# Cross-attention value product in 64x32 tiles over two PSUM banks, with new positions for feature-table, load and cross/FFN units

## The chip, the cores and the metric

One core of a Trainium2 chip runs the kernel; the other cores are idle. The metric is device microseconds (us) of one execution, and the time given for a kernel is the median of its executions. Engines: TensorE (PE; PEld is its weight load), VectorE (DVE), ScalarE (ACT), GpSimd (POOL) and SyncE (SP), which here only starts DMAs.

## The reference

One decoder layer on x of shape (4, 512, 256) in float32, with a context of 64 rows per batch part. Cut to what matters:

```python
def feature_map(x, fm_w, fm_b):                       # cross attention only
    z = einsum('nshd,ed->nshe', x, fm_w) + fm_b
    return concatenate([exp(z), exp(-z)], axis=-1)    # 16 -> 32 per head
def self_attention(x):                                # H=16 heads, key 16, value 64
    q = einsum('bnd,hkd->bnhk', x, query_proj); k = ...; v = ...
    attn = softmax(einsum('bnkh,bmhk->bnhm', q, k) / 4, axis=1)
    return einsum('bnhv,dhv->bnd', einsum('bnhm,bmhv->bnhv', attn, v), output_proj)
def cross_attention(ctx, query):                      # 16 heads of 16, 64 context rows
    v, k, q = (feature_map(t, fm_w, fm_b) for t in (ctx, ctx, query))
    attn = softmax(einsum('nqhd,nkhd->nhqk', q, k) / 16, axis=-1)
    out = einsum('nhql,nlhd->nqhd', attn, v)          # the product that is changed
    return out.reshape(N, S, 512) @ fc_w.T + fc_b
def ffn(x):                                           # x_prev is x shifted by one row
    xr = mu_r * x + (1 - mu_r) * x_prev; xk = mu_k * x + (1 - mu_k) * x_prev
    return sigmoid(xr @ W_r) * (relu(xk @ W_k) ** 2 @ W_v)
x = x + self_attention(layernorm(x))
x = x + cross_attention(ctx_1024, layernorm(x))
x = x + ffn(layernorm(x))
```

## The kernel before

**Units and orders.** The work is cut into units with a name, a batch part b (0 to 3) and arguments. Each engine runs its own list of units strictly in order, and the engines meet through semaphores. A list comes from hand-kept tables of slots: `orders()` gives each unit one slot per engine that has a share in it and sorts by slot. Self attention is 64 quads, q = 0 to 63, sixteen per batch part; a quad is two heads against half of the keys, its units have the slots 16q plus the numbers of `ATTENTION`: `scores` (PE), `max` (DVE), `exp` (four on ACT), `rsum` (DVE), `scale` (POOL, scales V by the row sums), `weigh` (PE, product with V), and for each second quad `ot_hi` (ACT) and `ot_lo` (DVE). Between them stand the other units. `PLAN` says where for every batch part (256 slots each; the offset -1 puts a unit of part b among the quads of part b+1), `FIRST` and `ONCE` for part 0's start, `LAST` for part 3's cross attention and FFN, which have no quads beside them, and `DEFER` for those units of part 2 that don't follow `PLAN`.

**Loads of the stacks.** q and k of a batch part are made in four `qk` units: (c, o) with c the half of the heads and o = 0 for q, 1 for k. PE makes one, ACT and DVE split it into a high and a low part in `qkt_hi`, `qkt_lo`, and SP writes both to DRAM (`q_parts`, `k_parts`; L547). From there `ld` (b, p) reads a stack of one pair of heads into `q_st` (L559) and `k_st` (two DMAs, L563). `scores` of an even quad waits for the stack n = q/2, so quads 14, 30, 46 and 62 wait for `ld` (b, 7). ACT's share of a `qk` unit waits until the q or k before it has been written out, as `qkt_hi` is one buffer. SP is in order too: if its next unit waits, all later DMAs wait behind it.

**Cross attention.** `t2` transposes the normalized rows, `z` and `xs` make features and scores with 64-row tiles of the array, two at a time into two PSUM banks; DVE takes maxima, ACT exp, DVE sums (`xn`), POOL scales, `pt` transposes (PE, then ACT copies to `pt_sb`). `pv` is the value product: `vblk` holds for a pair of heads a block-diagonal 128x64 matrix, so that one matmul serves two heads with 128 rows by 64 columns of the array, and two matmuls lie side by side in the columns. It is done per half of the rows and per group gg of heads. ACT (`oxt_hi`) and DVE (`oxt_lo`) split its result and `fc` multiplies it with the output weights.

**PSUM.** `scores` has four banks, `weigh` one (which has the same 128x64 tile form as `pv`), all other PE units go round the three left (seven when no scores are due); `bank_uses` deals them in PE's order.

**Feature tables.** `load("feat")` brings the small matrix and bias in ten DMAs; `feat` on DVE and ACT makes the signed table and its high and low parts. `cut` splits weights into high and low parts; the low part of the output weights, `cut("o")`, is made on POOL (L1319), and V of the second half of the heads may not be copied to `v_sb` before it, since the raw weights lie there.

## Time and profile before

| | |
|---|---|
| median of 3 executions | 479.99 us (479.38 to 481.4) |
| profiled execution, its own time | 479.61 us |
| span in the trace | 477.8 us |
| busy share of PE, DVE, ACT, POOL | 93%, 79%, 63%, 28% |
| scores of quads 0, 9, 28 and 63 start | 26.7, 67.5, 183.2 and 404.9 us |
| POOL first adds the `fc` bias | 122.3 us |

The span is the time from the first to the last instruction in the trace; 1.8 us of the execution's time lie around it. Times of rows are counted from the span's start. PE overlaps its matmuls, so a record's duration has some 0.17 us of latency that the next one doesn't add.

### The profile page before, as it was taken

What the parts mean: (1) busy time and instruction counts of PE and PEld (TensorE: products, weight loads), DVE (VectorE), ACT (ScalarE), POOL (GpSimd) and SP (SyncE); (2) the same over time, 40 slices, a digit from 0 to 9 for tenths busy, and PEclk for the clock granted to TensorE, in tenths of its full rate; (3) what the DMA queues carried; (4) which work ended last, traced back from release to release, by engine and by line L of the source; (5) the groups of instructions that cost most, each with busy time, mean ns of one, the idle gap of its engine ahead of it and who ended that gap; (6) DMA issues with size and microseconds to landing.
All of it is one profiled execution on the core that took longest, in us unless ns stands there. A gap on an engine that the chain in (4) does not pass through costs nothing.

```text
span 477.8 us, 7930 instructions
## 1 busy us (share of the span) xinstructions
PE 445.1 (93%) x2588; PEld 276.3 (58%) x2588; DVE 379.9 (79%) x689; ACT 299.0 (63%) x732; POOL 134.5 (28%) x181
## 2 busy tenths in 40 slices
PE   7779979999999999999999999999999999896985
PEld 3553426535655676557565675566556664485774
DVE  6567676786999988886999989777999787669664
ACT  4348866577688756565796856655796668323431
POOL 2511113113623351214431442114332413142410
PEclk9979999999999999999999999999999999897999
DMA  7852210133221001323301301333102000000001
GB/s 257 309 173 108 78 68 18 45 110 123 101 86 59 12 1 34 114 68 119 105 26 47 105 6 45 113 116 118 59 16 77 36 2 0 23 0 23 2 1 44
DMA packets 20013, 34.02 MB, mean 71 GB/s; under 512 B 2308, under 2 KB 6660, under 8 KB 19844
## 3 DMA queue, kind: packets, MB, share of 16 engines
q1 hardware_dynamic: 19972, 33.52, 21.5%
q8 instruction: 21, 0.34, 0.3%
q14 instruction: 20, 0.16, 0.1%
...
## 4 chain that ended last, share of the span: by engine, by line
PE 75%; DVE 9%; issue 5%; ACT 5%; DMA 3%; POOL 1%; SPq 0%; ACTq 0%; DVEq 0%; POOLq 0%
PE av_bank L653 18%; PE m_bank L591 9%; PE m_bank L593 7%; PE m_bank L592 7%; PE s_pair L639 7%; ACT e_sb L862 4%; DVE nmax L1060 3%; PE m_bank L782 3%; PE m_bank L831 3%; DMA q_parts<-qkt_lo 3%; PE m_bank L795 3%; PE m_bank L770 2%; PE m_bank L820 2%; PE av_bank L603 2%; PE m_bank L670 2%
## 5 line engine op out<-in xcount | busy, mean ns | idle before, releaser
L862 ACT ACTIVATE e_sb<-s_pair,nmax 128x512 f32<-128x512 f32 x256 | 172.8, 690 | 55.9 <-DVE nmax L1060 55.9
L1060 DVE TENSOR_REDUCE nmax<-s_pair 128x2 f32<-128x1024 f32 x128 | 152.9, 1214 | 20.2 <-PE s_pair L639 19.3
L653 PE MATMUL av_bank<-e_sb,v_sb 128*64 128x512 f32 x512 | 124.5, 607 | 4.5 <-POOL v_sb L1330 2.4
L1330 POOL TENSOR_TENSOR v_sb<-v_sb,rsum 128x256 f32<-128x256 f32 x64 | 39.6, 619 | 179.3 <-DVE rsum L1068 169.5
L653 PEld LDWEIGHTS av_bank<-e_sb,v_sb 128*64 128x64 f32 x512 | 31.6, 136 | 57.8 <-issue 46.6
L639 PE MATMUL s_pair<-q_st,k_st 64*128 64x512 f32 x256 | 50.6, 457 | 9.5 <-issue 6.8
L862 ACT ACTIVATION_READ_ACCUMULATOR e_sb<-s_pair,nmax 128x1 f32 x256 | 53.4, 208 | 0.0
L639 PEld LDWEIGHTS s_pair<-q_st,k_st 64*128 64x128 f32 x256 | 21.2, 186 | 55.3 <-issue 35.0
L1357 POOL TENSOR_TENSOR sx<-sx,xrec 128x512 f32<-128x512 f32 x24 | 24.8, 1043 | 46.4 <-DVE xrec L1240 46.4
L591 PE MATMUL m_bank<-wo_hi,ot_hi 128*128 128x256 f32 x120 | 34.9, 291 | 0.0
L593 PE MATMUL m_bank<-wo_lo,ot_hi 128*128 128x256 f32 x120 | 33.5, 279 | 0.0
L592 PE MATMUL m_bank<-wo_hi,ot_lo 128*128 128x256 f32 x120 | 33.5, 279 | 0.0
L875 ACT ACTIVATE ot_hi<-av_bank 128x512 fp32r<-128x512 f32 x32 | 19.3, 603 | 16.9 <-PE av_bank L653 16.8
L1068 DVE RECIPROCAL rsum<-esum 128x4 f32<-128x4 f32 x64 | 10.9, 170 | 22.1 <-ACT e_sb L862 21.4
L591 PE MATMUL m_bank<-wv_hi,xt_hi 128*128 128x512 f32 x62 | 27.9, 451 | 0.0
L591 PEld LDWEIGHTS m_bank<-wo_hi,ot_hi 128*128 128x128 f32 x120 | 22.5, 187 | 6.2 <-issue 6.1
L1339 POOL TENSOR_TENSOR rstd<-veps,power 128x2 f32<-128x2 f32 x24 | 16.7, 697 | 30.2 <-DVE veps L1124 30.2
L593 PE MATMUL m_bank<-wv_lo,xt_hi 128*128 128x512 f32 x62 | 25.0, 404 | 0.0
L592 PE MATMUL m_bank<-wv_hi,xt_lo 128*128 128x512 f32 x62 | 24.9, 402 | 0.0
L995 ACT ACTIVATE pt_sb<-m_bank 128x512 f32<-128x512 f32 x30 | 17.7, 598 | 10.3 <-PE m_bank L782 9.9
L1072 DVE TENSOR_TENSOR ot_lo<-av_bank,ot_hi 128x512 fp32r<-128x512 f32 x32 | 21.8, 681 | 1.7 <-ACT ot_hi L875 1.7
L592 PEld LDWEIGHTS m_bank<-wo_hi,ot_lo 128*128 128x128 f32 x120 | 22.5, 188 | 0.1
...
## 6 DMA issues: line engine op xcount, KB each, us to landing
...
```

The lines of the kernel that those rows point to most:

```text
L591: pe.matmul(dst, a_hi, b_hi, start=first, stop=False)
L592: pe.matmul(dst, a_lo, b_hi, start=False, stop=False)
L593: return pe.matmul(dst, a_hi, b_lo, start=False, stop=last)
L639: mm = pe.matmul(s_pair[i][:, par, :], k_st[at, n % STACK, m * P:(m + 1) * P], q_st[at, n % STACK, :], start=True, stop=True)
L653: mm = pe.matmul(av_bank[n % AV_BANKS][64 * par:64 * par + 64, :], v_sb[:, m, 2 * p + par, :], e_sb[:, (4 * q + 2 * i + par) % E_RING, :], ...
L862: act.activation(e_sb[:, g % E_RING, :], s_pair[k // 2][:, k % 2, :], ACT.Exp, bias=nmax[:, g % 8:g % 8 + 1], accum_out=esum[:, q % 4, k:k ...
L875: act.activation(ot_hi[:, n % 4, :], av_bank[n % AV_BANKS][:, :], ACT.Copy).then_inc(ot_hi_ready, 1)
L995: act.activation(pt_sb[:, 4 * gg:4 * gg + 4, (t % 2) * P:(t % 2 + 1) * P], bank(unit)[:, :].rearrange("p (i n) -> p i n", i=4), ACT.Copy)\
L1060: dve.tensor_reduce(nmax[:, at:at + 2], s_pair[i][:, :, :], AX_X, ALU.max, negate=True)\
L1072: dve.tensor_tensor(ot_lo[:, n % 4, :], av_bank[n % AV_BANKS][:, :], ot_hi[:, n % 4, :].bitcast(F32), ALU.subtract)\
L1330: pool.tensor_tensor(v_sb[:, m:m + 2, 2 * p:2 * p + 2, :], v_sb[:, m:m + 2, 2 * p:2 * p + 2, :], rsum[:, q % 4, :].rearrange("p (m h) -> p ...
L1357: pool.tensor_tensor(sx3, sx3, xrec[:, n % 4, :].unsqueeze(2).broadcast_to([P, 8, L]), ALU.mult)\
```

## The change

`pv` is done per half alone, in tiles of 64 rows by 32 columns: a head has its own 64x32 block of `vblk`, which no longer holds zeros, the heads of the upper 64 rows go to one bank and those of the lower 64 rows to another, and four column tiles lie side by side in each. So a half takes 16 matmuls of 64x32 in place of 8 of 128x64, and the unit waits for both banks and for all four `pt` copies of its half. The `fc` weights are permuted on the host to match. The filler matmuls (`warm`) at the start have 256 columns in place of 512. All tables have new slots. In the order of the units this does, beside many small swaps: `feat` goes from ahead of quad 0 to behind `max` of quad 4 on DVE; `load("rest")` (a batch part of x, biases, FFN weights, 1.4 MB) and `load("x1")` go from the start of SP's list to later places; `ld` (0, 2) comes before the DMAs of `qk` (0; 1, 0) and no longer after; `ld` (b, 7) comes behind the DMAs of `qk` (b+1; 0, 0) and no longer before; `cut("o")` goes behind `scale` of quad 2 on POOL; `ot_lo` goes ahead of both `max` units of its quad; `fv` (2, 0) goes behind `weigh` of quad 62 on PE; the fillers at the end are placed ahead of the last `xs` units. `DEFER` now lists all cross and FFN units of part 2.

```diff
...
 PLAN = [
-    ("qk", 0, (1, 0), dict(pe=5, act=1, dve=4, sp=14)),
...
-    ("kv", -1, (), dict(pe=-25, dve=-27)),
+    ("qk", 0, (1, 0), dict(pe=3, act=-3, dve=-3, sp=-7)),
...
+    ("kv", -1, (), dict(pe=-57, dve=-55)),
...
-    ("pv", -1, (0, 0), dict(pe=134, act=128, dve=125)),
...
-    ("pv", -1, (0, 1), dict(pe=136, act=129, dve=134)),
...
-    ("ld", 0, (7,), dict(sp=178)),
...
-    ("fk", -1, (0,), dict(pe=236, act=247, pool=239)),
-    ("qk", 1, (0, 0), dict(pe=206, act=207, dve=206, sp=230)),
...
-    ("qk", 1, (0, 1), dict(pe=223, act=221, dve=220, sp=235)),
...
+    ("pv", -1, (0, 0), dict(act=126, dve=123)),
...
+    ("pv", -1, (0,), dict(pe=134)),
+    ("pv", -1, (0, 1), dict(act=126, dve=129)),
...
+    ("ld", 0, (7,), dict(sp=219)),
...
+    ("fk", -1, (0,), dict(pe=227, act=234, pool=230)),
+    ("qk", 1, (0, 0), dict(pe=214, act=195, dve=211, sp=201)),
...
+    ("qk", 1, (0, 1), dict(pe=221, act=224, dve=223, sp=222)),
...
 LAST = [
...
-    ("pv", (0, 0), dict(pe=1081, act=1049, dve=1184)),
...
-    ("pv", (0, 1), dict(pe=1196, act=1152, dve=1231)),
...
+    ("pv", (0, 0), dict(act=1446, dve=1422)),
...
+    ("pv", (0,), dict(pe=2087)),
+    ("pv", (0, 1), dict(act=1452, dve=1437)),
...
 DEFER = [
...
-    ("fv", (0,), dict(pe=7, dve=-2, sp=5)),
...
+    ("op", (1, 0), dict(pe=-221, dve=-220)),
...
+    ("pv", (0, 0), dict(act=-122, dve=-116)),
...
+    ("pv", (0,), dict(pe=-117)),
+    ("pv", (0, 1), dict(act=-113, dve=-113)),
...
+    ("fv", (0,), dict(pe=15, dve=38, sp=15)),
...
 FIRST = [
-    ("warm", (0, 2), dict(pe=-1187)),
...
-    ("first", (0,), dict(pe=-282, act=-235, dve=-282)),
-    ("first", (1,), dict(pe=-126, act=-128, dve=-77)),
-    ("qk", (0, 0), dict(dve=-620, sp=-615, pe=-617, act=-561)),
-    ("qk", (0, 1), dict(pe=-376, act=-368, dve=-413, sp=-375)),
...
-    ("ld", (1,), dict(sp=-111)),
-    ("load", ("o",), dict(sp=-1334)),
-    ("ld", (2,), dict(sp=17)),
-    ("load", ("x1",), dict(sp=-1)),
-    ("load", ("fc",), dict(sp=-355)),
-    ("load", ("rest",), dict(sp=-2172)),
-    ("load", ("feat",), dict(sp=-822)),
...
+    ("warm", (0, 2), dict(pe=-210)),
...
+    ("first", (0,), dict(pe=-191, act=-194, dve=-181)),
+    ("first", (1,), dict(pe=-105, act=-103, dve=-116)),
+    ("qk", (0, 0), dict(dve=-842, sp=-229, pe=-155, act=-864)),
+    ("qk", (0, 1), dict(pe=-146, act=-151, dve=-149, sp=-140)),
...
+    ("ld", (1,), dict(sp=-130)),
+    ("load", ("o",), dict(sp=-1880)),
+    ("ld", (2,), dict(sp=-12)),
+    ("load", ("x1",), dict(sp=174)),
+    ("load", ("fc",), dict(sp=-773)),
+    ("load", ("rest",), dict(sp=259)),
+    ("load", ("feat",), dict(sp=-1357)),
...
 ONCE = [
-    ("cut", ("o",), dict(act=-195, pool=-202)),
...
-    ("feat", (), dict(dve=-190, act=-192)),
-    ("kf", (0,), dict(pe=57, act=73)),
...
-    ("warm", (3, 1), dict(pe=1751)),
-    ("warm", (4, 1), dict(pe=2626)),
...
+    ("cut", ("o",), dict(act=14, pool=52)),
...
+    ("feat", (), dict(sp=87, dve=84, act=83)),
+    ("kf", (0,), dict(pe=156, act=149)),
...
+    ("warm", (3, 1), dict(pe=1903)),
+    ("warm", (4, 1), dict(pe=3038)),
...
-ATTENTION = dict(scores=12, weigh=42, max=(11, 12), exp=(17, 17, 18, 18), rsum=27, scale=22, ot_hi=39, ot_lo=44)
+ATTENTION = dict(scores=13, weigh=42, max=(11, 11), exp=(16, 16, 17, 17), rsum=26, scale=15, ot_hi=36, ot_lo=43)
...
 def bank_units(name, b, args):
-    if name in ("xs", "z"):
+    if name in ("xs", "z", "pv"):
...
-        vblk = sb("vblk", [P, NP, 2 * FE])
+        vblk = sb("vblk", [P, NP, FE])
...
-                cols = 512 if at < 3 else 256
+                cols = 256
...
-                    pe.matmul(av_bank[0][:, 0:cols], id_sb[:, :] if at >= 3 else vblk[:, 0:2, :].rearrange("p a b -> p (a b)"),
+                    pe.matmul(av_bank[0][:, 0:cols], id_sb[:, :] if at >= 3 else vblk[:, 0:4, :].rearrange("p a b -> p (a b)"),
...
-            def pv(b, half, gg):
-
-                unit = ("pv", b, (half, gg))
-                wait_bank(pe, unit)
+            def pv(b, half):
+
+                units = bank_units("pv", b, (half,))
+                for unit in units:
+                    wait_bank(pe, unit)
...
-                    wait_emptied(pe, ("pt", b, (t, gg)))
+                    for gg in range(2):
+                        wait_emptied(pe, ("pt", b, (t, gg)))
...
-                    for q in range(2):
-                        pair = 4 * gg + 2 * i + q
-                        mm = pe.matmul(bank(unit)[64 * q:64 * q + 64, i * HALF:(i + 1) * HALF], vblk[:, pair, :],
-                                       pt_sb[:, pair, :], start=True, stop=True)
-                mm.then_inc(filled[uses[unit][0]], 1)
+                    for c in range(4):
+                        for r, unit in enumerate(units):
+                            rows = slice(64 * r, 64 * r + 64)
+                            mm = pe.matmul(bank(unit)[32 * c:32 * c + 32, i * HALF:(i + 1) * HALF],
+                                           vblk[rows, 4 * i + c, :], pt_sb[rows, 4 * i + c, :], start=True, stop=True)
+                            if (i, c) == (1, 3):
+                                mm.then_inc(filled[uses[unit][0]], 1)
...
-                    wait_filled(act, ("pv", pb, (ph, gg)))
+                    for r in range(2):
+                        wait_filled(act, ("pv", pb, (ph, r)))
...
-                    wait_filled(dve, ("pv", b - 1, (1, 1)))
+                    for r in range(2):
+                        wait_filled(dve, ("pv", b - 1, (1, r)))
...
-                    ins = dve.tensor_copy(to[64 * q:64 * q + 64, :, :, q * FE:(q + 1) * FE],
+                    ins = dve.tensor_copy(to[64 * q:64 * q + 64, :, :, :],
...
-    wfc = np.asarray(L0_xattn_fc_w).T.reshape(2, 2, 2, 2, FE, D).transpose(2, 0, 1, 3, 4, 5).reshape(H * FE, D)
+    wfc = np.asarray(L0_xattn_fc_w).T.reshape(4, 2, 2, FE, D).transpose(2, 1, 0, 3, 4).reshape(H * FE, D)
...
```

## Rows read from the trace of the kernel before

**Rows 1.** The page: busy time of the engines (share of the span) and records.

```profile
PE 445.1 (93%) x2588; PEld 276.3 (58%) x2588; DVE 379.9 (79%) x689; ACT 299.0 (63%) x732; POOL 134.5 (28%) x181
```

**Rows 2.** Busy time by stretch: stretch, length, engines, PE clock, DMA share, GB/s.

```profile
5.00:10.00 5.00, 5.00 (x15) 2.41 (x14) 3.71 (x14) 2.36 (x5) 1.43 (x2) 1.00 0.95 350
...
45.00:90.00 45.00, 39.60 (x198) 19.84 (x192) 31.50 (x51) 32.37 (x90) 8.99 (x15) 1.00 0.14 47
...
180.00:285.00 105.00, 104.89 (x642) 66.09 (x641) 91.03 (x168) 71.27 (x180) 32.99 (x46) 1.00 0.22 71
```

**Rows 3.** Waits of PE from 90 to 390 us: total, times, longest; the longest line.

```profile
PE m_bank L770 <- issue: 0.6, 1, 0.6
```

**Rows 4.** Timeline of PE: a 64-row unit, the V product, scores.

```profile
128.48 1.16 PE L770 MATMUL m_bank<-kblk,qf 64*128 64x128 f32 x16
129.57 1.94 PE L653 MATMUL av_bank<-e_sb,v_sb 128*64 128x512 f32 x8
131.44 0.73 PE L639 MATMUL s_pair<-q_st,k_st 64*128 64x512 f32 x4
```

**Rows 5.** Timeline: a value product (one half) and the V product behind it.

```profile
164.66 2.04 PE L795 MATMUL m_bank<-pt_sb,vblk 128*64 128x256 f32 x16
...
166.50 1.92 PE L653 MATMUL av_bank<-e_sb,v_sb 128*64 128x512 f32 x8
```

**Rows 6.** Timeline of SP in part 1: the second q write.

```profile
187.59 0.61 SPq L547 DMA_DIRECT2D q_parts<-qkt_lo  x1
```

**Rows 7.** Busy time by stretch, chosen for DMA traffic (share and GB/s at the end).

```profile
150.10:151.30 1.20, 1.20 (x12) 0.75 (x11) 1.20 (x2) 1.20 (x3) 0.35 (x1) 1.00 0.00 0
151.30:158.50 7.20, 6.42 (x52) 3.75 (x49) 6.66 (x11) 5.31 (x14) 1.04 (x1) 1.00 0.23 75
...
188.10:192.00 3.90, 3.90 (x22) 2.33 (x19) 3.79 (x12) 2.22 (x6) 1.26 (x2) 1.00 0.46 134
...
197.00:211.00 14.00, 14.00 (x66) 8.69 (x65) 10.06 (x14) 8.30 (x22) 2.22 (x3) 1.00 0.22 72
```

**Rows 8.** Timeline of PE: scores of quad 30, and of quad 14.

```profile
195.12 1.11 PE L639 MATMUL s_pair<-q_st,k_st 64*128 64x512 f32 x4
...
97.90 0.51 PE L639 MATMUL s_pair<-q_st,k_st 64*128 64x512 f32 x2
```

**Rows 9.** Timeline of SP from 86 to 108 us: the first q write of part 1.

```profile
90.11 0.63 SPq L547 DMA_DIRECT2D q_parts<-qkt_hi  x1
```

**Rows 10.** Timeline of the start, all engines.

```profile
20.17 4.50 POOL L1319 TENSOR_TENSOR wo_lo<-v_sb,wo_hi 128x2048 fp32r<-128x2048 f32 x1 [1.11 <-ACT wo_hi L905]
...
20.82 3.94 DVE L1173 TENSOR_SCALAR fm_sb<-fm_sb 128x128 f32<-128x128 f32 x1 [2.89 <-DMA fm_sb<-in_fm_t]
...
26.74 1.22 PE L639 MATMUL s_pair<-q_st,k_st 64*128 64x512 f32 x4 [6.17 <-issue]
...
28.25 0.60 SPq L547 DMA_DIRECT2D q_parts<-qkt_lo  x1
...
38.03 0.61 ACT L930 ACTIVATE qkt_hi<-m_bank 128x512 fp32r<-128x512 f32 x1
...
39.51 0.69 ACT L862 ACTIVATE e_sb<-s_pair,nmax 128x512 f32<-128x512 f32 x1 [0.87 <-DVE nmax L1060]
```

**Rows 11.** Timeline of PE at the end of the quads.

```profile
406.04 1.99 PE L842 MATMUL m_bank<-wffn_sb,kact 128*128 128x256 f32 x8
...
411.87 2.58 PE L653 MATMUL av_bank<-e_sb,v_sb 128*64 128x512 f32 x8 [1.98 <-POOL v_sb L1330]
414.38 3.00 PE L831 MATMUL m_bank<-mix_k,wffn_sb 128*128 128x256 f32 x8
```

**Rows 12.** Busy time by stretch: the clock there.

```profile
412.90:416.40 3.50, 3.50 (x11) 1.70 (x8) 1.20 (x3) 0.60 (x1) 0.00 (x0) 0.52 0.00 0
```

**Rows 13.** Timeline of ACT: the two halves of the first value product of part 3.

```profile
446.94 0.60 ACT L1006 ACTIVATE oxt_hi<-s_pair 128x512 fp32r<-128x512 f32 x1 [0.89 <-PE s_pair L795]
447.81 0.60 ACT L1006 ACTIVATE oxt_hi<-s_pair 128x512 fp32r<-128x512 f32 x1 [0.27 <-PE s_pair L795]
```

More of the change, by code:

```diff
@@ new lines @@
+    ("pt", -1, (3, 1), dict(pe=183, act=171)),
+    ("ln1", 1, (0,), dict(dve=178, pool=160)),
+    ("pv", -1, (1, 0), dict(act=178, dve=184)),
+    ("ln3", -1, (0,), dict(dve=171, pool=180)),
+    ("ld", 0, (6,), dict(sp=175)),
+    ("pv", -1, (1,), dict(pe=186)),
+    ("pv", -1, (1, 1), dict(act=178, dve=184)),
+    ("t1", 1, (0,), dict(pe=190, act=188, dve=193)),
+    ("mix", -1, (0,), dict(dve=206)),
+    ("t3", -1, (0,), dict(pe=205, act=194)),
+    ("ln1", 1, (1,), dict(dve=182, pool=161)),
@@ new lines @@
+    ("xs", (0, 0), dict(dve=516, act=445)),
+    ("z", (1, 0), dict(act=366)),
+    ("xs", (0,), dict(pe=971)),
+    ("xs", (0, 1), dict(dve=523, act=539)),
+    ("xn", (0, 0), dict(dve=1307, pool=34)),
+    ("xs", (1,), dict(pe=1084)),
+    ("xs", (1, 1), dict(dve=1051, act=1040)),
+    ("xn", (1, 0), dict(dve=1321, pool=1301)),
+    ("xn", (0, 1), dict(dve=1309, pool=34)),
+    ("z", (1,), dict(pe=1380)),
+    ("z", (1, 1), dict(act=444)),
+    ("xs", (1, 0), dict(dve=554, act=570)),
+    ("xn", (1, 1), dict(dve=1352, pool=1301)),
@@ new lines @@
+    ("xs", (2, 0), dict(dve=1308, act=1312)),
+    ("pt", (0, 0), dict(pe=2052, act=606)),
+    ("pt", (0, 1), dict(pe=2056, act=1364)),
+    ("xs", (2,), dict(pe=2005)),
+    ("xs", (2, 1), dict(dve=1308, act=1444)),
+    ("xn", (2, 0), dict(dve=1354, pool=1345)),
+    ("xs", (3,), dict(pe=2032)),
+    ("xs", (3, 1), dict(dve=1389, act=1510)),
+    ("pt", (1, 1), dict(pe=2087, act=1430)),
+    ("xn", (2, 1), dict(dve=1389, pool=1392)),
+    ("xs", (3, 0), dict(dve=1372, act=1491)),
+    ("pt", (1, 0), dict(pe=2064, act=1395)),
@@ new lines @@
+    ("z", (0,), dict(pe=-196)),
+    ("z", (0, 1), dict(act=-195)),
+    ("z", (0, 0), dict(act=-197)),
+    ("xs", (0, 0), dict(dve=-186, act=-187)),
+    ("z", (1, 0), dict(act=-158)),
+    ("t2", (1,), dict(pe=-162, act=-163, dve=-162)),
+    ("xn", (0, 0), dict(dve=-181, pool=-168)),
+    ("xs", (1, 0), dict(dve=-177, act=-173)),
+    ("xs", (0,), dict(pe=-188)),
+    ("xs", (0, 1), dict(dve=-185, act=-181)),
+    ("xn", (1, 0), dict(dve=-154, pool=-163)),
+    ("pt", (1, 0), dict(pe=-133, act=-132)),
@@ new lines @@
+    ("xn", (0, 1), dict(dve=-160, pool=-166)),
+    ("z", (1,), dict(pe=-149)),
+    ("z", (1, 1), dict(act=-155)),
+    ("pt", (0, 0), dict(pe=-142, act=-155)),
+    ("xs", (1,), dict(pe=-175)),
+    ("xs", (1, 1), dict(dve=-170, act=-167)),
+    ("pt", (1, 1), dict(pe=-126, act=-132)),
+    ("xn", (1, 1), dict(dve=-153, pool=-153)),
+    ("xn", (2, 0), dict(dve=-135, pool=-138)),
+    ("xs", (2,), dict(pe=-140)),
+    ("xs", (2, 1), dict(dve=-146, act=-129)),
+    ("pt", (0, 1), dict(pe=-141, act=-150)),
@@ new lines @@
+    ("pt", (3, 0), dict(pe=-88, act=-94)),
+    ("pt", (3, 1), dict(pe=-88, act=-94)),
+    ("pv", (1, 0), dict(act=-94, dve=-79)),
+    ("pv", (1,), dict(pe=-75)),
+    ("pv", (1, 1), dict(act=-81, dve=-79)),
+    ("fc", (0,), dict(pe=-94, dve=-95)),
+    ("ln3", (0,), dict(dve=-91, pool=-92)),
+    ("mix", (0,), dict(dve=-61)),
+    ("t3", (0,), dict(pe=-70, act=-72)),
+    ("ln3", (1,), dict(dve=-27, pool=-28)),
+    ("fc", (1,), dict(pe=-66, dve=-39)),
+    ("t3", (1,), dict(pe=-6, act=-6)),
@@ new lines @@
+    ("warm", (1, 2), dict(pe=-2414)),
+    ("warm", (2, 2), dict(pe=-2370)),
+    ("ln1", (0,), dict(dve=-2197, pool=-2055, do=-2061)),
+    ("ln1", (1,), dict(dve=-2108, pool=-2000, do=-2059)),
+    ("cut", ("first",), dict(act=-2072, dve=-2059)),
+    ("cut", ("qk",), dict(act=-2049, dve=-2000)),
+    ("t1", (0,), dict(dve=-2058, pe=-2091, act=-2057)),
+    ("t1", (1,), dict(pe=-2035, act=-2041, dve=-2054)),
+    ("first", (0,), dict(pe=-191, act=-194, dve=-181)),
+    ("first", (1,), dict(pe=-105, act=-103, dve=-116)),
@@ L230 @@
+    ("v", (0, 1), dict(pe=19, dve=21)),
+    ("v", (0, 2), dict(pe=-108, act=-126)),
+    ("v", (0, 3), dict(pe=32, dve=34)),
 ]
 ONCE = [
[L233 to L241 removed]
```

292 lines of the change are left out of this document (127 added, 165 removed).

## The prediction, made before the change was run

> **What bounds the kernel now.** The page first: PE is busy for 93% of the span, DVE for 79%, ACT for 63% [rows 1]. The average hides stages, so the second view is busy time by stretch: from 180 to 285 us, a whole part of the batch, PE is busy for 104.9 of 105 us, DVE for 91.0; in part 0 (45 to 90 us) PE has 39.6 of 45 [rows 2]. The view of waits says the same: from 90 to 390 us the longest entry of PE is 0.6 us [rows 3]. So in parts 1 to 3 whatever PE saves comes off the end, whatever PE is made to wait goes onto it, and no other engine matters until it makes PE wait. The start and the end of the span are chains of waits and are read from timelines.
>
> **1. The value product.** One half has 16 matmul records in a group of 2.04 us, and the V product behind it ends at 168.42, 1.72 us after the end of the value product [rows 5]; it has four rounds of two records side by side with 512 columns, so a round of 512 columns takes 0.43 and one of 256 takes 0.215. The value product has eight rounds now: 1.72 us. If eight 64x32 tiles run side by side, its 32 records are four rounds: 0.86. That saves 0.86 us per half, and the six halves of parts 0, 1 and 2 lie beside quads, in the PE-bound stretch: -5.2. The two of part 3 lie in the end, where the next step is ACT's copy. Now the first group is copied at 446.94 while PE makes the second, copied at 447.81 [rows 13]; afterwards both banks are full only at the end of the unit and the copies follow one another, so fewer rounds are paid back by less overlap: 0, between -0.5 and +0.9 a half. Bounds of the whole term: -5.2 if eight run together, 0 if four do. Two side by side in the columns are seen for the value product, two in the rows for `xs` [rows 4, 5]; eight are seen nowhere. I take eight, since both directions work one by one and nothing in the rows shows them competing.
>
> **2. Changes of tile form.** A group with 64-row tiles ends at 129.64 and the V product after it at 131.51, 1.87 us later [rows 4], against 1.72 where the value product with the same form stood ahead [rows 5]: 0.15 us for the change. Scores after it end at 132.17, 0.66 later, of which 0.43 are their two rounds: 0.23. The value product has a form of its own now, so it can't share one with `weigh`. Putting both orders side by side from the tables, PE changes form 213 times from quad 0 to quad 62 before and 207 times after, because more units of one form stand together: six fewer at 0.18 is -1.1. Bounds -1.4 and 0. The Trainium skill (TensorEngine Tiling (Array Packing), section Tiling Modes) says that a change of mode drains the engine; by that rule a form used by one unit alone is a cost, and the 0.15 to 0.23 us here agree with it.
>
> **3. The last stack of each part.** `ld` (b, 7) goes behind the two q writes of the next part. What it then costs is seen from three things. First, when SP can issue: it is in order, and the second q write of part 2 goes out at 187.59 [rows 6]; its two writes move from 188.1 to 192.0. Second, how long a stack takes: alone, from issue at 150.1, nothing moves for 1.2 us and then data moves for 7.2 us; two stacks close behind each other take 14.0 [rows 7]. So 7.0 each, and it follows at 192.0: it lands at 199.0, and at about 199.5 because `t3` now stands ahead of that `qk` unit on PE. Third, when it is needed: quad 30's scores start at 195.12 [rows 8]; with `fk` moved in ahead (a group of eight such records is about 1.9 us, as in [rows 11]) and the short `kv` moved out (about 0.5) at 196.4. PE waits 3.1 us, and everything behind it on PE too: it is in order, and this stretch has no idle time to give. The same for quad 46: 6.2 together. For quad 14 the first q write goes out at 90.11 [rows 9]: traffic from 91.3, 3.9 for the writes and 7.0 for the stack, 102.2 against 97.90 [rows 8]; 4.3, of which I take 4.0, as part 0 has idle time of its own. Sum +10.2. Before, this load was issued long ahead (at 150.1 for a need at 195.1), so it is covered fully now. Bounds: 0, if the stack needn't wait behind the writes, and +15, if each wait also lets PE's clock fall: a wait of 1.98 us at 409.9 was followed by 3.4 us at half clock [rows 11, 12], worth up to 1.7 us each.
>
> **4. The start.** Now DVE's step of `feat` takes 3.94 us beside POOL's 4.50 us step of `cut("o")`, the unit `first` (0, 1) waits behind it, and PE idles 6.17 us, to 26.74 [rows 10]. With `feat` gone that idle time goes too, and quad 0 starts some 6 us sooner. I don't expect it to last. ACT's share of `qk` (0; 1, 1) stands between the exps of quads 1 and 2 and can't start until the q write of `qk` (0; 1, 0) has landed. Now that write is issued at 28.25 and ACT gets to the unit at 38.03 without waiting [rows 10], so it landed between about 33 (4.7 us after its issue, as in [rows 6, 7]) and 38. Afterwards the stack `ld` (0, 2) is ahead of it: +7.0 [rows 7]. What is taken out ahead of it is 1.4 + 0.5 MB, at 350 GB/s [rows 2] 5.5 us. So it lands between 34.5 and 39.5, and the exps of quad 2 start at 35 to 40 where they started at 39.51: about -1.5 from there. Against it stand two things. The low part of the output weights (4.50 us on POOL) comes behind quad 2's `scale`, and DVE's copy of `v` (0; 1, 1), with the maxima of quad 4 behind it, waits for it: about +1.3. And `feat` on DVE and ACT, which wait for each other there, stands in the loop of quad 4: about +1.2. Together +1.0; bounds -6.2 (the idle time is gained for good) and +3.
>
> **5. The end of the quads.** `weigh` of quad 63 waits 1.98 us for POOL, the clock falls, and `fk` takes 3.00 us where a like group takes 1.99 [rows 11, 12]. With `fv` (2, 0) in that gap PE idles less; the chain to `weigh` itself is unchanged. If the clock stays up: 1.0 for `fk` and 0.6 for `weigh` (2.58 against 1.94, [rows 4]); I take -1.5, bounds -1.6 and 0. In part 3's cross attention the fillers no longer stand between the `pt` units but ahead of them, which frees the path but may leave the clock low: -0.5, bounds -2 and +2.
>
> Edits with no cost of their own: `load("rest")` is needed by POOL at 122.3 us and would be issued at about 110, behind the writes of `qk` (1; 1, 0); it has slack as long as it moves at the 350 GB/s of [rows 2] (4 us). The narrower fillers and `ot_lo` ahead of `max` move work by tenths.
>
> **Sum.** -5.2 - 1.1 + 10.2 + 1.0 - 1.5 - 0.5 = +2.9, against the profiled execution's 479.6 (477.8 in the span and 1.8 around it; the median of the runs is 0.4 higher): **482.5 us**.
>
> **Rivals.** *B, the stacks come in time.* It decides at the 3.1 us of quad 30: if a stack behind a q write lands within 8 us of the second write's issue and not 11.9, term 3 is zero and the time 482.5 - 10.2 = 472.3. For it: 16 DMA engines are only 22% busy while a stack moves [rows 7], so a second transfer could run beside it. Against it: two stacks took 14.0, exactly twice one. *C, the tiles don't pack.* If records of the value product follow one another as those of `xs` do, 16 in the 1.09 us from 128.48 to 129.57 [rows 4], 32 take 2.2 us, no less than now: term 1 becomes about +0.5, the time 488.2. For it: no row shows more than two at once. Against it: both pairings that the rows show, two in the columns and two in the rows, run at the full rate of a round. The Trainium skill (TensorE: Matmul & The Clock Gate, section "Wait — 56ns, not 53.3ns?") says that with its hardware decoder off PE spends about 62 ns on each matmul; by that rule 32 records take 1.98 us and nothing is saved. The rows of `xs`, at 68 ns each, don't exclude it. *D, the start is kept.* If the q write lands by 34 us and POOL's step disturbs nobody, term 4 is -6.2 and the time 475.3; it decides at the start of quad 2's exps. *That the change doesn't do what it says* is part of C.
>
> **Chances.** Forecast 0.45, with its own range of 479 to 488 (upwards the falls of the clock); B 0.22; C 0.13; D 0.14; mixtures 0.06. About 0.5% is what a measurement of this kernel can tell from no change, so faster is below 477.6 and slower above 482.4. B, most of D and half the mixtures are faster: 0.37. Of the forecast's case a good half is above 482.4, and all of C: 0.41. Same: 0.22. The range that leaves out 2 in 10, both ends between the cases: 470 to 488.
>
> **What would show it.** Term 1: the value product as one group of 32 records with a length near 1.1 us. Term 3: PE idle for 3 to 4 us ahead of the scores of quads 14, 30 and 46, while the DMA traffic of a stack ends just there; if PE's row has no such gaps, B holds. Term 4: quad 0 at about 20 us, but quad 4 no sooner than 45. Term 5: full clock from 405 to 420. The prediction is wrong if those gaps are absent or if quad 9 starts more than 3 us sooner than its 67.5 now.

## The result, and the profile after

The changed kernel takes 504.94 us (median of 4, 504.74 to 506.4) against 480.06 us before (median of 4): a ratio of 1.052, with a 95% interval of 1.049 to 1.055. That is 25 us slower; 482.5 was forecast, with a range of 470 to 488. The execution that was profiled took 506.4 us, 504.6 of them in the span. Medians are of all executions of a kernel, but ratios leave out an execution that ran slow at a lower clock, which here is one of ten with stack and start put back.

The page has the engines' busy time (answers to [rows 1]):

```profile
PE 443.5 (88%) x2716; PEld 275.2 (55%) x2716; DVE 376.6 (75%) x689; ACT 298.9 (59%) x732; POOL 134.8 (27%) x181
```

PE has a little less work than before (443.5 us against 445.1, although part of it ran at half clock) in a span that is 26.8 us longer. So PE waits more. The view of PE's waits from 90 to 390 us, where the largest line was 0.6 us before [rows 3], has

```profile
PE s_pair L690 <- issue: 19.0, 4, 5.9
PE s_pair L690 <- ACT e_sb L917: 1.4, 2, 0.7
PE m_bank L642 <- DVE ot_lo L1128: 0.7, 1, 0.7
```

Four waits of `scores` hold 19.0 us. The timeline of PE shows two of them, quads 14 and 30 (answers to [rows 8]):

```profile
109.53 1.22 PE L690 MATMUL s_pair<-q_st,k_st 64*128 64x512 f32 x4 [5.91 <-issue]
...
217.12 1.22 PE L690 MATMUL s_pair<-q_st,k_st 64*128 64x512 f32 x4 [5.50 <-issue]
```

The other two are quad 46 and quad 18:

```profile
329.04 1.22 PE L690 MATMUL s_pair<-q_st,k_st 64*128 64x512 f32 x4 [5.60 <-issue]
...
134.17 0.73 PE L690 MATMUL s_pair<-q_st,k_st 64*128 64x512 f32 x3 [2.04 <-issue]
```

"issue" names no releaser. What was under way is seen on SP, ahead of quad 30 (answers to [rows 6]):

```profile
205.47 0.61 SPq L598 DMA_DIRECT2D q_parts<-qkt_lo  x1
206.19 0.56 SPq L610 DMA_DIRECT2D q_st<-q_parts  x1
206.79 1.20 SPq L614 DMA_DIRECT2D k_st<-k_parts  x2
```

The q write goes out, the stack of `ld` (1, 7) right behind it, and the scores start 11.65 us after the second write. Now the stretches (stretch, length, engines, PE clock, DMA share, GB/s; the second and fourth line answer to [rows 2]):

```profile
34.00:39.00 5.00, 0.08 (x2) 0.00 (x0) 0.38 (x1) 0.00 (x0) 0.24 (x1) 1.00 0.13 51
45.00:90.00 45.00, 39.90 (x185) 19.58 (x184) 29.21 (x49) 30.12 (x83) 11.99 (x15) 0.91 0.17 53
107.40:114.20 6.80, 4.67 (x12) 2.64 (x14) 2.36 (x2) 2.58 (x8) 0.00 (x0) 0.50 0.19 64
180.00:285.00 105.00, 98.38 (x623) 61.01 (x622) 84.44 (x157) 68.37 (x171) 31.52 (x44) 0.97 0.18 59
211.60:216.60 5.00, 0.02 (x2) 0.00 (x0) 1.47 (x3) 1.82 (x5) 1.61 (x2) 1.00 0.54 186
216.60:223.50 6.90, 6.38 (x18) 3.63 (x20) 2.53 (x3) 2.79 (x8) 0.61 (x1) 0.51 0.10 32
405.00:420.00 15.00, 15.00 (x123) 9.16 (x123) 10.19 (x18) 8.73 (x22) 2.99 (x5) 1.00 0.07 27
```

In each gap PE stands empty, at full clock at first, and then come some 7 us at half clock (1.2 in place of 2.4 GHz): the granted clock is 0.50 and 0.51 there. At quads 14 and 30 the clock falls 2.1 and 0.5 us before the scores start (107.4 and 216.6), at quad 46 3.2 us before. So the gap is paid for a second time in part, by the work behind it at half clock.

```profile
325.90:329.00 3.10, 0.00 (x0) 0.00 (x0) 0.00 (x0) 0.00 (x0) 0.84 (x1) 0.50 0.50 183
```

The Trainium skill (TensorE: Matmul & The Clock Gate, section Part 1: The HAM clock gate) says that the clock goes to half when PE has not been busy and comes back with work; the trace agrees with that order of events.

The start, as a timeline (answers to [rows 10]):

```profile
20.04 0.73 PE L690 MATMUL s_pair<-q_st,k_st 64*128 64x512 f32 x4 [0.21 <-issue]
...
28.31 1.26 SPq L598 DMA_DIRECT2D q_parts<-qkt_lo  x1
...
39.89 0.60 ACT L985 ACTIVATE qkt_hi<-m_bank 128x512 fp32r<-128x512 f32 x1 [8.90 <-DMA q_parts<-qkt_lo]
40.39 0.68 ACT L917 ACTIVATE e_sb<-s_pair,nmax 128x512 f32<-128x512 f32 x1
...
41.88 0.80 PE L690 MATMUL s_pair<-q_st,k_st 64*128 64x512 f32 x2 [7.80 <-ACT e_sb L917]
...
44.03 4.54 POOL L1376 TENSOR_TENSOR wo_lo<-v_sb,wo_hi 128x2048 fp32r<-128x2048 f32 x1
...
48.67 0.69 DVE L1212 COPY v_sb<-m_bank 128x512 f32<-128x512 f32 x1 [2.03 <-POOL wo_lo L1376]
...
68.11 0.49 PE L690 MATMUL s_pair<-q_st,k_st 64*128 64x512 f32 x2 [0.77 <-ACT e_sb L917]
```

Quad 0 starts at 20.0 and not at 26.7. But ACT stands still for 8.90 us until the low q write has landed, with the exps of quad 2 behind it, and PE for 7.80 us with quad 3. From 39.1 to 49.4 us the clock is at half, 2.7 us of it in the gap.

The value product itself did what the change was to do. The groups of PE's value product (shapes, records, busy time, mean ns; the two forms are those among and behind the quads), and one half with the V product behind it (answers to [rows 5]):

```profile
L849 PE MATMUL m_bank<-pt_sb,vblk 64*32 64x256 f32 x192 | 6.6, 381 | 0.8 <-ACT pt_sb L1051 0.5 <-issue 0.3
...
L849 PE MATMUL s_pair<-pt_sb,vblk 64*32 64x256 f32 x64 | 2.2, 381 | 1.8 <-ACT pt_sb L1051 1.8
```

```profile
167.15 1.10 PE L849 MATMUL m_bank<-pt_sb,vblk 64*32 64x256 f32 x32 [0.28 <-ACT pt_sb L1051]
168.17 1.94 PE L704 MATMUL av_bank<-e_sb,v_sb 128*64 128x512 f32 x8
```

Starts of `scores` in us, from the timelines of PE:

| quad | 0 | 4 | 9 | 13 | 14 | 29 | 30 | 33 | 45 | 46 | 63 |
|---|---|---|---|---|---|---|---|---|---|---|---|
| before | 26.7 | 46.2 | 67.5 | 91.9 | 97.9 | 189.2 | 195.1 | 213.5 | 293.7 | 299.7 | 404.9 |
| after | 20.0 | 49.9 | 74.7 | 97.9 | 109.5 | 204.3 | 217.1 | 239.5 | 316.1 | 329.0 | 433.2 |
| stack ahead | 20.8 | 50.6 | 75.4 | 98.7 | 104.3 | 196.0 | 203.2 | 223.8 | 300.4 | 307.6 | 410.7 |
| all three put back | 20.2 | 43.7 | 68.5 | 91.7 | 97.4 | 189.0 | 196.3 | 216.2 | 292.8 | 300.0 | 402.6 |

The last two rows are experiments. After minus before, from unrounded starts, is +7.1 at quad 9 and grows by 5.7, 6.9 and 6.9 at quads 14, 30 and 46; 1.3 of the 6.9 is work that now stands there, since with the stack ahead quad 30 comes 7.2 us behind quad 29 where it came 5.9 behind before. What the half clock costs is seen against the row with the stack ahead: the quad behind each gap takes 1.2, 1.8 and 1.1 us longer. It is least at quad 46, where the clock was down for 3.2 us of the gap itself.

### The profile page after: what moved, and what is told of

It is laid out like the page before. It is cut to its first block, busy times and chain, and to the rows that moved or that the text cites. A ratio compares the mean times of both kernels' runs of the same rounds, so it can differ in the third digit from the quotient of the medians.

```text
span 504.6 us, 8181 instructions
## 1 busy us (share of the span) xinstructions
PE 443.5 (88%) x2716; PEld 275.2 (55%) x2716; DVE 376.6 (75%) x689; ACT 298.9 (59%) x732; POOL 134.8 (27%) x181
## 4 chain that ended last, share of the span: by engine, by line
PE 57%; DVE 17%; issue 10%; DMA 7%; ACT 6%; POOL 1%; SPq 1%; ACTq 0%; DVEq 0%; POOLq 0%
PE av_bank L704 15%; PE m_bank L642 7%; PE m_bank L643 6%; PE m_bank L644 6%; DVE nmax L1116 5%; PE s_pair L690 5%; ACT e_sb L917 4%; DMA q_st<-q_parts 3%; DMA q_parts<-qkt_lo 3%; PE m_bank L833 2%; PE m_bank L821 2%; PE m_bank L721 2%; PE m_bank L875 2%; PE m_bank L897 2%; PE m_bank L886 1%
## 5 line engine op out<-in xcount | busy, mean ns | idle before, releaser
L1116 DVE TENSOR_REDUCE nmax<-s_pair 128x2 f32<-128x1024 f32 x128 | 150.2, 1215 | 28.6 <-PE s_pair L690 28.5
L704 PE MATMUL av_bank<-e_sb,v_sb 128*64 128x512 f32 x512 | 127.8, 621 | 4.9 <-POOL v_sb L1387 2.5
L690 PEld LDWEIGHTS s_pair<-q_st,k_st 64*128 64x128 f32 x256 | 21.4, 191 | 74.5 <-issue 49.4
L642 PE MATMUL m_bank<-wv_hi,xt_hi 128*128 128x512 f32 x62 | 29.1, 470 | 0.6 <-DVE qkt_lo L1199 0.6
L644 PE MATMUL m_bank<-wv_lo,xt_hi 128*128 128x512 f32 x62 | 26.2, 422 | 0.0
L643 PE MATMUL m_bank<-wv_hi,xt_lo 128*128 128x512 f32 x62 | 26.1, 421 | 0.0
L642 PEld LDWEIGHTS m_bank<-wo_hi,ot_hi 128*128 128x128 f32 x120 | 23.2, 193 | 4.7 <-issue 4.6
L644 PEld LDWEIGHTS m_bank<-wo_lo,ot_hi 128*128 128x128 f32 x120 | 23.2, 194 | 0.0
## 6 DMA issues: line engine op xcount, KB each, us to landing
x_sb<-in_x SPq DMA_DIRECT2D x3, 512.0 KB, 12.1
```

The costliest lines, as they stand in the source:

```text
L642: pe.matmul(dst, a_hi, b_hi, start=first, stop=False)
L643: pe.matmul(dst, a_lo, b_hi, start=False, stop=False)
L644: return pe.matmul(dst, a_hi, b_lo, start=False, stop=last)
L690: mm = pe.matmul(s_pair[i][:, par, :], k_st[at, n % STACK, m * P:(m + 1) * P], q_st[at, n % STACK, :], start=True, stop=True)
L704: mm = pe.matmul(av_bank[n % AV_BANKS][64 * par:64 * par + 64, :], v_sb[:, m, 2 * p + par, :], e_sb[:, (4 * q + 2 * i + par) % E_RING, :], ...
L1116: dve.tensor_reduce(nmax[:, at:at + 2], s_pair[i][:, :, :], AX_X, ALU.max, negate=True)\
```

## The experiments

The theory: the loss is SP's queue. A stack read issued right behind the q writes lands 11.6 us after them; at quads 14, 30 and 46 PE has nothing else, and the clock falls; at the start the order is the other way round, a write behind a stack, and ACT waits. The rival: the new slots as a whole are worse, another engine is late at each of these places, and taking one wait away only shows the next.

### The loads

**Stack ahead of the writes.** One slot of the changed kernel.

```diff
-    ("ld", 0, (7,), dict(sp=219)),
+    ("ld", 0, (7,), dict(sp=200)),
```

> The changed kernel with one slot altered: ld (b, 7) goes ahead of the two q writes of qk (b+1; 0, 0) on SP again (sp 219 to 200). Theory: the three gaps of 5.9, 5.5 and 5.6 us ahead of the scores of quads 14, 30 and 46 (17.0 together) are the stack's 7 us behind the writes, and each made the clock fall for 6.83 us, which costs up to 3.4 more. So all three gaps and the half clock behind them vanish: 505 - 17.0 - (3 to 10) = 478 to 485. Rival: the new order of DVE, ACT and POOL is late at these places as well and takes over the wait; then less than 10 is gained (above 495) and PE waits for e_sb or nmax where it waited for the stack.

482.01 us (median of 10), ratio to before 1.0044 (1.0014 to 1.0074): 22.9 us of the 25. All three gaps are gone (table), and the one of 2.04 us ahead of quad 18 is down to 0.86. In the two profiled executions the stretch from quad 9 to quad 62 takes 354.7 and 331.5 us. Of these 23.2 us, 17.2 are at the three quads, 4.1 in the quad behind each (the half clock) and 1.9 around quad 18. The rival is out as an account of the loss: PE's largest line of waits from 90 to 390 us is now

```profile
PE s_pair L690 <- ACT e_sb L917: 3.0, 5, 0.8
```

It was 1.4 us in the changed kernel, so a small part of what is taken away does come back as another wait.

**The same in the kernel before.** One slot of the kernel before, nothing else.

```diff
-    ("ld", 0, (7,), dict(sp=178)),
+    ("ld", 0, (7,), dict(sp=231)),
```

> The kernel before with one slot altered: ld (b, 7) goes behind the two q writes of qk (b+1; 0, 0) (sp 178 to 231), nothing else. Theory: a stack issued right behind the writes lands 11.4 to 11.6 us after the second write's issue (11.6 measured twice in the changed kernel). With the write at 187.59 it lands at 199.1 where the scores of quad 30 started at 195.1: a gap of 4.0, the same for quad 46, and 4.4 for quad 14: 12.4 us, and 1.1 to 1.9 for the clock behind each: 480 + 16 to 18 = 496 to 498. Rival: the wait was an effect of the changed kernel's later q writes and its other slots; then the gaps are under 2 us here, the clock stays up, and the time is under 487.

494.7 us, ratio 1.033 (1.027 to 1.039). The waits of PE from 90 to 390 us and quad 30 on the timeline:

```profile
PE s_pair L639 <- DMA k_st<-k_parts: 12.3, 3, 4.3
```

```profile
207.62 0.94 PE L639 MATMUL s_pair<-q_st,k_st 64*128 64x512 f32 x3 [3.98 <-DMA k_st<-k_parts]
```

Here the trace names the releaser, the stack's DMA. The gaps are 4.27, 3.98 and 4.08 us, 12.3 together, where 12.4 were worked out from the 11.6 us: this part of the arithmetic is right to 0.1 us. The median is 1.3 us below the expected range; the profiled execution (499.9 us, granted clock 0.962) was the slowest of the four, and the others had 0.972 to 0.976. This run also says that the loss doesn't need the changed kernel's tiles or its other slots.

**The write sooner.** In the changed kernel DVE's share of `qk` (b+1; 0, 0) goes back ahead of `mix` (b, 0).

```diff
-    ("qk", 1, (0, 0), dict(pe=214, act=195, dve=211, sp=201)),
+    ("qk", 1, (0, 0), dict(pe=214, act=195, dve=205, sp=201)),
```

> The changed kernel with one slot altered: DVE's share of qk (b+1; 0, 0) goes ahead of mix (b, 0) again (dve 211 to 205, mix at 206). Theory: the q writes of quad 28's loop went out 7.1 us behind its scores where they had gone out 4.4 behind before, and 2.4 of that are the three steps of mix (0.68, 0.89 and 0.88 us) ahead of qkt_lo on DVE. So the gaps ahead of quads 30 and 46 shrink from 5.5 to 3.1 to 3.3 (the size that the prediction gave), the one ahead of quad 14 stays at 5.9 (no mix there): 505 - 4.6 to -6 = 499 to 500.5. Rival: the stack's landing is set by its own transfer and the loads behind it, the gaps stay above 5 and the time within 1 us of 505.

497.11 us, 7.8 less than the changed kernel. The gaps at quads 30 and 46 are 3.09 and 2.67, the one at quad 14 is 6.46. On DVE, in the changed kernel and then in this one:

```profile
199.38 2.36 DVE L1116 TENSOR_REDUCE nmax<-s_pair 128x2 f32<-128x1024 f32 x2
201.66 0.68 DVE L1321 TENSOR_TENSOR mix_k<-xt 128x512 f32<-128x512 f32 x1
202.37 0.89 DVE L1323 SCALAR_TENSOR_TENSOR mix_r<-mix_k,mu_sb,xt 128x256 f32<-128x256 f32 x2
203.29 0.88 DVE L1327 SCALAR_TENSOR_TENSOR mix_k<-mix_k,mu_sb,xt 128x256 f32<-128x256 f32 x2
204.09 0.69 DVE L1199 TENSOR_TENSOR qkt_lo<-m_bank,qkt_hi 128x512 fp32r<-128x512 f32 x1
```

```profile
198.30 0.69 DVE L1199 TENSOR_TENSOR qkt_lo<-m_bank,qkt_hi 128x512 fp32r<-128x512 f32 x1
198.91 0.68 DVE L1321 TENSOR_TENSOR mix_k<-xt 128x512 f32<-128x512 f32 x1
```

ACT's part of the same `qk` unit ran at 201.17 in the changed kernel; DVE took up its own at 204.09, behind three steps that nobody waited for. A swap of two units on an engine that PE doesn't wait for cost 2.4 and 2.9 us at these gaps, through SP's queue. The three gaps are 4.8 us less in all. The whole is 7.8, more than the 4.6 to 6 expected: quad 9 comes 2.0 us sooner, though the edit touches nothing ahead of it. There the changed kernel's profile has 3.4 us at half clock (69.9 to 73.3 us) that this one hasn't, so these 2.0 may be chance and not the edit. The last 1.0 isn't taken apart.

### The start

**Write first.**

```diff
-    ("ld", (2,), dict(sp=-12)),
+    ("ld", (2,), dict(sp=17)),
```

> The changed kernel with one slot altered: ld (0, 2) goes behind the q writes of qk (0; 1, 0) on SP again (sp -12 to 17), as before the change. Theory: the gap of 7.8 us ahead of the scores of quad 3 (34.1 to 41.9) is ACT waiting for that write, which landed at 39.8 behind the 7 us of the stack; without the stack ahead it lands at about 33, the gap shrinks to 1 us or less and quad 4 starts 5 to 7 us sooner, and the clock does not fall at 39: 505 - 6 = 497 to 500. Rival: the start is bound by POOL's low part of the output weights and by feat in the loop of quad 4, so quad 9 starts no more than 2 us sooner and the time is above 502.

500.51 us, 4.4 less than the changed kernel and 0.5 above the expected range; quad 3 starts at 36.5 and not at 41.9, quad 9 at 69.5 and not at 74.7. That the clock wouldn't fall was wrong: it is at half from 37.4 to 44.3 us, 6.8 us in place of 10.2. ACT gets the write's landing some 6.4 us sooner (timeline of ACT in the next run, which has the same start):

```profile
33.50 0.60 ACT L985 ACTIVATE qkt_hi<-m_bank 128x512 fp32r<-128x512 f32 x1 [2.58 <-DMA q_parts<-qkt_lo]
```

**Combinations of the edits above:** stack and start; stack, start and `qk`; stack and `qk`.

> Both slots altered together. If the two causes are independent their gains add: 505 - 23 (-18 to -30) = 475 to 487. If the new order itself costs something elsewhere (x loads shared with the stack of quad 18, other late engines), the time stays above 485.

> The changed kernel with three slots put back: the stack ahead of the writes, the start's write ahead of its stack, DVE's share of qk ahead of mix. Theory: the late q write cost only what the stack behind it cost; with no stack queued behind it, 2.4 us more or less of it are hidden: within 1 us of the run with the first two alone (479.6). Rival: the late write also holds up the stack of quad 16 or ACT's next share of qk, and this is 2 us or more faster.

> The changed kernel with two slots put back (the stack ahead of the writes, DVE's share of qk ahead of mix), the start left as changed. It completes the set: stack alone 482.0, stack and start 479.6, all three 476.0. Theory A: the start's write costs what the pair without it showed, 2 to 4.5 us, so this is 478 to 480.5. Rival: with the stack ahead the start's 7.6 us gap is all that is left and shows in full: 482 or more.

| put back | us | ratio to before (95%) |
|---|---|---|
| nothing | 504.94 | 1.052 (1.049 to 1.055) |
| start | 500.51 | 1.044 (1.040 to 1.048) |
| stack | 482.01 | 1.004 (1.001 to 1.007) |
| stack, qk | 481.18 | 1.001 (0.999 to 1.003) |
| stack, start | 479.58 | 0.999 (0.996 to 1.002) |
| stack, start, qk | 475.96 | 0.992 (0.989 to 0.994) |

With three slots put back the new kernel is faster than the one before, by 0.8%. The rows ran in different series, whose own medians of the kernel before lie between 479.56 and 480.54 us, so they are compared by their ratios. The start's order then costs 0.8% with nothing else put back, 0.55% with the stack and 0.95% with stack and `qk`: 3.7, 2.6 and 4.6 us, of which the intervals (some 2 us on each difference) leave open whether they differ. The third slot was expected to give less than 1 us once no stack waits behind the write; by the ratios it gave 1.6 us without the start's slot and 3.6 with it, again with some 2 us of interval on each. That the second is above 1 us is shown, that the two differ is not. Where it comes from isn't explained: in the profiled executions the spans of the two kernels differ by 1.1 us (476.0 and 474.9). An execution's time goes with its granted clock (476.3 us at 0.987, 480.2 at 0.978 for the kernel with two slots). Open.

**feat alone.** The kernel before with `feat` later.

```diff
-    ("feat", (), dict(dve=-190, act=-192)),
-    ("kf", (0,), dict(pe=57, act=73)),
-    ("kf", (1,), dict(pe=163, act=165)),
+    ("feat", (), dict(dve=84, act=83)),
+    ("kf", (0,), dict(pe=156, act=149)),
+    ("kf", (1,), dict(pe=164, act=164)),
```

> The kernel before with only feat moved (dve -190, act -192 to 84, 83) and kf, which needs it (pe 57, act 73 to 156, 149). Theory: the 6.17 us idle ahead of quad 0 go and quad 0 starts at about 20.6, but the q write of qk (0; 1, 0) and the loop of quads 1 to 9 (max, exps, scores wait for one another) take most of it back: quad 9 is 0 to 3 us sooner than 67.5 and the time 477 to 480. Rival (D of the prediction, start kept): quad 9 at 62 and 474; rival the other way: with feat and kf among the quads it is slower than before.

481.53 us, ratio 1.0034 (0.9999 to 1.0068). Quad 0 starts 5.2 us sooner, quad 4 1.0 sooner, quad 10 1.7 later. The idle 6 us ahead of quad 0 were no loss, only the place where PE waited; the rival in which their end is a gain for good is out. At quad 9 0.8 us were left, within the 0 to 3 expected; then `kf`'s work on PE, which has moved behind quad 9, takes them back. The time was expected at 477 to 480 and is above it. The other rival, that the move makes the kernel slower, is neither shown nor excluded: its interval begins just below 1.

### The tiles alone

The kernel before with nothing but the tiles. What is left to choose is where the merged unit and its copies go; five placings were run. The fillers at the start have 256 columns and `LAST` has the like edit in all; the edits from the second placing on are in short form, with `pv` left out. First, all at the old slots, the PE unit at those of the second old one:

```diff
-    ("pv", -1, (0, 0), dict(pe=134, act=128, dve=125)),
-    ("pv", -1, (0, 1), dict(pe=136, act=129, dve=134)),
-    ("pv", -1, (1, 0), dict(pe=156, act=154, dve=158)),
-    ("pv", -1, (1, 1), dict(pe=169, act=169, dve=168)),
+    ("pv", -1, (0, 0), dict(act=128, dve=125)),
+    ("pv", -1, (0,), dict(pe=136)),
+    ("pv", -1, (0, 1), dict(act=129, dve=134)),
+    ("pv", -1, (1, 0), dict(act=154, dve=158)),
+    ("pv", -1, (1,), dict(pe=169)),
+    ("pv", -1, (1, 1), dict(act=169, dve=168)),
```

> The kernel before with only the value product in 64x32 tiles over two banks (one PE unit per half, at the slot of the second old one); all other slots are those of before, fillers at the start 256 columns. Theory (term 1 of the prediction, borne out by 8.8 us busy for 256 records against 16.5 for 128): 480 - 5.2 = 474 to 476. Rival: the form that only this unit uses adds drains, or the later copies of both banks hold up ACT, and it is within 1 us of before.

Second, from the first:

```diff
-    (0,): pe=136; (0, 0): act=128, dve=125; (0, 1): act=129, dve=134; fc (0): pe=141, dve=145
+    (0,): pe=139; (0, 0): act=136, dve=136; (0, 1): act=137, dve=137; fc (0): pe=143, dve=147
-    (1, 0): act=154, dve=158; (1, 1): act=169, dve=168
+    (1, 0): act=170, dve=170; (1, 1): act=171, dve=171
```

> The kernel before with the value product in 64x32 tiles as in the run before, but with its units some slots later in PLAN: the first half's PE unit behind weigh (pe 136 to 139), its copies on ACT and DVE at 136 and 137 (they were at 125 to 134, ahead of a quad's exps), fc at 143, the second half's copies at 170 and 171. Theory: the 6.7 us lost there came from ACT and DVE that stood still for the merged unit (1.94 and 1.30 us) while exps and gate waited behind them, and PE then waited 2.1 us for gate; placed later the waits go and the 5.2 us show: 475 to 480. Rival: the merged unit's two banks held at once in a ring of three are what makes PE wait, and the time stays above 483.

Third, from the first:

```diff
-    (0, 0): act=128, dve=125; (0, 1): act=129, dve=134; xs (3): pe=136; xn (2, 1): dve=135
+    (0, 0): act=129, dve=128; (0, 1): act=129, dve=129; xs (3): pe=139; xn (2, 1): dve=133
-    (1,): pe=169; (1, 0): act=154, dve=158; (1, 1): act=169, dve=168
+    (1,): pe=170; (1, 0): act=177, dve=172; (1, 1): act=177, dve=173
```

> The kernel before with the tiles alone, third placing: the first half's unit at pe 136 directly behind fv, weigh and only then xs (3) (136 to 139), so that the unit neither waits for a bank nor makes xs wait for one; its copies on ACT at 129 (behind two of a quad's exps) and on DVE at 128 and 129, behind gate; xn (2, 1) one slot ahead of xs (3); the second half's unit behind weigh at 170, copies at 177 on ACT and 172, 173 on DVE. Theory: the two placings before lost what they lost to waits of 1.0, 1.0 and 0.9 us a part (bank, POOL, pt_sb) or 2.1 and 0.9 (gate, pt_sb); without them the 0.86 us per half show: 480.5 - 5 = 474 to 477. Rival: in this order of units some engine always has to wait for a merged unit, and the time stays at or above that of before.

Fourth, from the third:

```diff
-    (1, 0): act=177, dve=172; (1, 1): act=177, dve=173
+    (1, 0): act=171, dve=172; (1, 1): act=171, dve=173
```

> The third placing of the tiles with one thing mended: ACT's two copies of the second half's product go from slot 177, where PE's op (0, 1) had to wait 3.78 us a part for the bank that they hold, to 171. Theory: the waits before op (0, 1) go (11.3 us) and with them the falls of the clock; quads 24, 40 and 56 were reached 0.9 to 1.4 sooner already, so the second half adds its 0.86: 480 - 3 = 475 to 479, with 1.1 us a part left for a late ot_lo. Rival: the second half's unit and its copies make other engines late again, and the time stays above 481.

Fifth, from the fourth:

```diff
-    (1, 0): act=171, dve=172; (1, 1): act=171, dve=173
+    (1, 0): act=171, dve=170; (1, 1): act=171, dve=170
```

> The placing before with DVE's two copies of the second half at 170, ahead of the row sums and maxima of the next quad, and no longer at 172 and 173 behind them, where DVE first waited 2.62 us for that quad's scores and PE then 2.82 us for the bank. Theory: with the 8.4 us of these waits gone the saving of term 1 shows beside the waits that are left (1.1 for ot_lo, 0.7 for POOL a part): 480 - 1 to -4 = 476 to 479. Rival: a third engine takes over the wait, and tiles in this order of units save nothing: 480 or more.

Medians: 486.27, 484.39, 499.45, 494.27 and 482.22 us, ratios 1.015, 1.009, 1.041, 1.027 and 1.005 (1.003 to 1.008). The expectation failed five times, although PE's work fell as said: 6.6 us for the 192 records among the quads, where 96 took 12.6 before. From quad 9 to quad 62 the profiled executions take 6.0, 4.2, 18.9, 14.8 and 1.6 us longer than before (in the first, third and fourth another 2.0 to 2.5 us are lost ahead of quad 9, where no value product stands and the clock is at half for 3.4 us). Each placing had another wait. In the first DVE waited 1.30 us for ACT's copy with `gate` behind it, and PE 2.06 us for `gate`. In the second PE waited for a second free bank, as the merged unit needs two of three (1.02 us), for POOL and for `pt_sb`. In the third and fourth the copies came too late for `op` (0, 1), which needs their bank; waits of the fourth, whole span:

```profile
PE m_bank L595 <- DVE oxt_lo L1199: 8.4, 3, 2.8
```

The fifth has from 90 to 390 us

```profile
PE av_bank L657 <- DVE ot_lo L1081: 3.3, 3, 1.1
PE m_bank L786 <- POOL sx L1367: 2.3, 4, 0.7
PE m_bank L802 <- ACT pt_sb L1004: 1.2, 1, 1.2
```

Its quads 24, 40 and 56 start 0.9, 1.4 and 1.4 us sooner, counted against the quad before, and the two quads behind each give back 1.6: the tiles' gain is there and is taken back, 1.1 of it each time by the wait for a late `ot_lo` on DVE (busy 91 of 105 us). That is read from the trace; no run moves `ot_lo`, so whether the tiles alone can be made to pay in the old order stays open.

## Why the prediction was wrong

**Term 3 (+10.2) is the step that failed, in size.** It measured 22.9 us, above its upper bound of 15. The place (quads 14, 30, 46) and the cause were right, and so was the length of the queue: 11.4 us from the second write's issue to landing, where 11.6 to 11.7 were seen. It was off in two things. "Its two writes move from 188.1 to 192.0" took over the time at which SP could issue from the kernel before. The new DVE order has `mix` ahead of `qkt_lo`, so the write went out 7.1 us behind the scores of quad 28 and no longer 4.4, and the gaps were 5.5 and 5.6 in place of 3.1; with `mix` behind it again they were 3.09 and 2.67.

The falls of the clock were put in the bound, at up to 1.7 each, and not in the sum, though the wait of 1.98 us that the prediction itself cites had been followed by half clock. Of the 22.9, 17.0 are the three gaps and some 4 the half clock.

At quad 14 the second write went out at 97.81, 5.8 us ahead of the point where PE had nothing else (103.62); before it had gone out 7.2 ahead of the scores. 11.7 - 5.8 is the gap of 5.9, against the 4.0 forecast.

The rest is around quad 18, and there a cost was put at nothing: `load("rest")` "has slack", but on SP it stands right ahead of the stack of quad 18. That stack is issued at 128.10 us, while 247 GB/s move from 124 to 132, and the scores start at 134.17, 2.04 us late; with the stack of quad 14 ahead, everything there is some 6 us sooner and 0.86 is left. No run moves this load, so its part is argued from the order.

**Term 4 (+1.0) failed too.** The landing came at 39.8, at the upper end of its bounds (34.5 to 39.5) and 0.3 beyond; the middle was taken. The lower bound rested on 4.7 us from issue to landing. With the write first (stack and start put back) it was issued at 24.48 and ACT started at 33.50, 9.0 us later, so 4.7 doesn't hold beside the stacks of the start. The exps of quad 2 then began 0.9 us later than before and not 1.5 sooner. `wo_lo` was priced at 1.3 and cost DVE 2.03. The clock that the 7.8 us gap would bring down wasn't priced: half clock for 10.2 us. Quad 9 came 7.1 us later than before; putting the write first gave 2.6 to 4.6 us back in time. What else holds up the start is open; some 2 of the 7.1 may be the chance stretch of half clock named above. The rival D is out.

**Term 1 (-5.2): the work fell, the time didn't.** One half is 1.10 us where it was 2.04 (1.1 was forecast). Up to the end of the V product behind it the two take 2.96 us where they took 3.76, so 0.80 are saved per half where 0.86 was forecast; the rest is the change of form, 1.86 us from the end of the value product to the end of the V product where it was 1.72. The length fits eight tiles running together, and rival C is out: 32 records in 1.10 us are 34 ns each. The Trainium skill (TensorE: Matmul & The Clock Gate, section "Wait — 56ns, not 53.3ns?") has 62 ns for a matmul without the hardware decoder; the measurement excludes that for these tiles. But "in parts 1 to 3 whatever PE saves comes off the end" was wrong. In the order of before a unit that needs all four copies and two banks at once made PE wait for as much as it saved, or more, in each of the five placings. In the new order (stack and start put back) PE is busy for 292.6 of the 300 us from 90 to 390, where it was 297.2 before: there is more waiting than before, 2.9 of it for exps. From quad 9 to quad 62 it takes 1.8 us less than before, and 3.0 less with `qk` put back too, where terms 1 and 2 had 6.3. How much of these 3.0 us is the tiles and how much the order isn't taken apart.

**Term 2 (-1.1)** wasn't measured by itself; the 0.15 us for a change of form holds (0.14 here). **Term 5 (-1.5)**: from the scores of quad 63 to the end of `fk` 12.1 us where it was 12.5; `fk` ran at full clock (1.99 us, not 3.00), but `weigh` waits for `ot_lo` and POOL ahead of it. The tail gained 1.1, where 0.5 was forecast.

**Rival B** is out: no stack behind a write was in time. Its condition, a landing within 8 us of the second write's issue, could have been ruled out from the rows: a stack alone took 8.4 us from its issue (150.1 to 158.5) [rows 7], and here it is issued 0.7 us after the write. Behind the writes it took 10.9 from its issue (206.19 to 217.12). So the writes ahead add some 2.5 us to its transfer; the other 3.0 of the 5.5 us at quad 30 are there because it is issued so late.

What the prediction named to tell right from wrong held: gaps at the three places, quad 0 at 20.0 and quad 4 at 49.9 (no sooner than 45), full clock from 405 to 420. The gaps had been given as 3 to 4 us and were 5.5 to 5.9. The profiled execution is 23.9 us above its forecast (506.4 against 482.5), and the starts of the quads say where: 6.1 up to quad 9 (term 4), 17.5 from there to quad 62, and 0.3 behind it. Of the 17.5, some 13 are term 3 (23.2 against 10.2), and 4.4 the tiles and the new order, which saved 1.9 us with the stack ahead and not the 6.3 of terms 1 and 2.
